# The cosine product of the keys' rotation: kept in PSUM, with the bank released by the sum

## The chip, the cores and the metric

The kernel runs on one core of a Trainium2 chip. The metric is the device time of one execution in microseconds; the median of three executions stands for the kernel. One execution was also taken with the hardware profiler, and all rows below are of that one.

## What is computed

The block is a gated cross-attention layer followed by a small expert layer. Only the first matters here. With `x` of 8 batches x 56 tokens x 512 and a context of 8 x 1500 x 512, it computes

```
q = layernorm(x) @ wq          # 32 heads of 128
k = context @ wk               # 8 key heads of 128, each shared by 4 query heads
v = context @ wv
q, k = rope(q), rope(k)        # rope(x) = x * cos + rotate_half(x) * sin
p = softmax(q @ k^T / sqrt(128) + mask)
x = x + tanh(g) * ((p @ v) @ wo)
```

`rotate_half` swaps the two halves of 64 of a head's 128 numbers; the sign sits in the sine table. So for each batch and each key head the kernel needs `k * cos + swapped(k) * sin` on 128 x 1500 numbers, the head's dimension on the partitions and the context's positions on the columns. All is in fp32.

## The kernel before, in words

**Precision by halves.** Each fp32 operand of a matmul is split in a high part (a rounded copy) and a low part (the rest). A product is three matmuls: high x high, low x high, high x low (`PASSES`). So every tensor that TensorE reads needs a copy by ACT (the high part) and a subtraction by DVE or POOL (the low part).

**Stages.** First the queries of all heads are computed and written to DRAM. Then comes the attention stage, which takes most of the time: 8 batches x 8 key heads ("groups"). At last the output projection and the expert layer.

**One step of the attention stage** handles group g of batch b. TensorE does the scores of group g (`S0` to `S5`: two halves of the query rows x three chunks of 500 positions), the transposes of the probabilities (`T0` to `T5`), their product with the values (`PV0` to `PV5`), and between them, for the next group, the keys (`K00` to `K23`: three chunks, each in four parts of three matmuls) and parts of the values (`V..`). In the last group of a batch, the "turn", the context of the next batch is transposed too (`C0` to `C11`).

The order of the pieces is written out by hand, one string for each engine: `PE_STEP`, `ACT_STEP`, `DVE_STEP`, each with a form for even groups (0, 2, 4, 6), odd groups (1, 3, 5), the turn (7), the last step of all, and the first keys. The engines run through their own strings in order and meet only at semaphores. In eight batches there are 32 even steps, 24 odd steps and 7 turns.

**The keys of one chunk** (an "item"; 3 per group, numbered through the whole kernel, `s` is the item's number modulo 2):

1. TensorE (`k_part`, line 805) makes twelve matmuls into PSUM bank `k_banks[:, s]`. There are two such banks (`RING = 2`), so item n uses the bank of item n-2. Ahead of an item's first matmul stands `pe.wait_ge(k_free, item + 1)`.
2. ACT (`k_exchange`, line 715) copies the two halves of the bank, swapped, to `k_swap[:, s]` in SBUF.
3. DVE (`k_cos_part`, line 938) multiplies the bank by the cosine table into `k_rot[:, s]` in SBUF, and signals `k_free`: from here on the bank may be written again. Since it writes `k_rot[:, s]`, it first waits until POOL has read that buffer for item n-2 (`k_lo`).
4. DVE (`k_sin_part`, line 942) multiplies `k_swap[:, s]` in place by the sine table.
5. DVE (`k_rotate`, line 948) adds the two in SBUF, and signals `k_rotated`.
6. ACT (`k_high`, line 720) makes the high part, POOL (`k_low`, line 673) the low part. The scores of the next step (line 845) wait for `k_lo`.

In the profile both `k_swap` and `k_rot` bear the name of the buffer that holds them, `k_work`; the key banks, the score banks and the value banks are all called `low_banks`.

In the strings, `K20` is the first part of chunk 2, so it is the one that reuses the bank of the same group's chunk 0. On TensorE it stands behind `K13` in odd steps (`... K11 K12 K13 K20 ...`), behind `K13 V40` in even ones and behind `K12 K13 T0 T1` in the turn. On DVE the words `cos0 sin0 rot0` are the three operations of chunk 0.

**The query part** rotates its queries in another way (lines 503, 505 and 508): the cosine product is written in place into its PSUM bank, and the sum reads that bank and the sine product in SBUF.

**The output projection** reuses the key banks; its first piece (`O0`) waits for the last keys' bank.

Of the kernel before, what the change touches and what calls it, by code (L numbers as in the profile page):

```python
# [27 lines left out]
SC = 500  # L28
NC = SK // SC
# [8 lines left out]
RING = 2  # L38
# [51 lines left out]
DVE_STEP = {  # L90
# [11 lines left out]
def step_kind(g, last):  # L102
    return ("last" if last else "turn") if g == HKV - 1 else ("odd" if g % 2 else "even")
# [6 lines left out]
def tasks(order):  # L110

    for word in order.split():
        what = word.rstrip("0123456789")
        digits = word[len(what):]
        numbers = tuple(int(x) for x in digits) if what in ("K", "V") else (int(digits),) if digits else (0,)
        yield what, numbers
# [7 lines left out]
def t_place(kind, what, n):  # L124

    fills = t_fills(PE_STEP, kind)
    assert fills == t_fills(ACT_STEP, kind) == t_fills(DVE_STEP, kind)
    assert t_fills(ACT_STEP, "pre") == t_fills(ACT_STEP, "even")
    return fills.index((what, n))
# [7 lines left out]
def k_item(b, g, c=0):  # L137

    return b * K_ITEMS + g * NC + c


def sv_item(b, g, i=0):

    return b * SV_ITEMS + (V_AHEAD + (g // 2) * (2 * SCORES + VT) + (g % 2) * (SCORES + V_REST) + i)


def v_fill(g, m):

    return m - (0 if g % 2 else V_AHEAD)
# [7 lines left out]
def c_item(b, m):  # L157

    return b * T_ITEMS + (NT + (HKV - 1) * PT + t_place("turn", "C", m))
# [367 lines left out]
def attention_part(nc, ctx, query, shared, cT, ctx_in, mask, wo, q_dram, inv_dram, attn_dram):  # L527
    ident, stage, w, tables, mask_t = shared.ident, shared.stage, shared.w, shared.tables, shared.mask_t
# [8 lines left out]
    def sem(name):  # L537
        return ctx.enter_context(nc.semaphore(name))

    def halves(name, shape):  # L540
# [5 lines left out]
    k_swap, k_rot = (shared.k_work[:, n * 2 * SC:(n + 1) * 2 * SC].rearrange("p (s n) -> p s n", s=2) for n in range(2))  # L546
# [11 lines left out]
    k_banks, sv_banks = shared.low_banks[:, 0:RING], shared.low_banks[:, RING:2 * RING]  # L558
# [2 lines left out]
    q_loaded = [sem(f"q_loaded{i}") for i in range(2)]  # L561
    sp_passed, dve_passed = sem("sp_passed"), sem("dve_passed")
    sv_ready, sv_free, v_hi = sem("sv_ready"), sem("sv_free"), sem("v_hi_ready")
    k_ready, k_swapped, k_free, k_sined, k_rotated, k_hi, k_lo = (
        sem(n) for n in ("k_ready", "k_swapped", "k_free", "k_sined", "k_rotated", "k_hi_ready", "k_lo_ready"))
    t_ready, t_hi, t_free = sem("t_ready"), sem("t_hi_ready"), sem("t_free")
    o_ready, o_lo_copied, o_free, attn_ready = sem("o_ready"), sem("o_lo_copied"), sem("o_free"), sem("attn_ready")
    inv_stored, inv_loaded = sem("inv_stored"), sem("inv_loaded")
# [227 lines left out]
    def _(pe):  # L796
        def k_part(item, s, g, c, d, context_item):

            if d == 0:
                pe.wait_ge(k_free, item + 1)  # L800
                if context_item is not None:

                    pe.wait_ge(t_free, context_item + (RING + 1))
            for n, (a, m) in enumerate(PASSES):
                mm = nc.tensor.matmul(k_banks[:, s, 0:SC], w[0][a][:, d, g * DH:(g + 1) * DH],  # L805
                                      cT[m][:, d, c * SC:(c + 1) * SC], start=(d == 0 and n == 0),
                                      stop=(d == DC - 1 and n == len(PASSES) - 1))
            if d == DC - 1:
                mm.then_inc(k_ready, 1)

        def v_part(item, g, m, t, context_item):

            if t == 0:
                pe.wait_ge(sv_free, item + 1)
            if context_item is not None:

                pe.wait_ge(t_free, context_item + (RING + 1))
            tile = 2 * m + t
            for d in range(DC):
                for n, (a, mv) in enumerate(PASSES):  # L820
                    mm = nc.tensor.matmul(sv_banks[0:ST, m % 2, t * PAIR:(t + 1) * PAIR],  # L821
                                          cT[a][:, d, tile * ST:(tile + 1) * ST], w[1][mv][:, d, g * DH:g * DH + PAIR],
                                          start=(d == 0 and n == 0), stop=(d == DC - 1 and n == len(PASSES) - 1))
            if t == 1:
                mm.then_inc(sv_ready, 1)

        def c_transposes(b, item, s, m):

            pe.wait_ge(t_free, item + 1)
            c_stage_ready(pe, b, m)  # L830
            for d in range(DC):
                mm = nc.tensor.transpose(t_banks[:, s, d * ST:(d + 1) * ST], c_tile(m)[:, d * P:(d + 1) * P],
                                         ident[0:ST, 0:ST])
            mm.then_inc(t_ready, 1)

        def scores(b, g, i):

            h, c = divmod(i, NC)
            if i == 0:
                pe.wait_ge(q_lo, b * HKV + (g + 1))  # L840
            pe.wait_ge(sv_free, sv_item(b, g, i) + 1)
            if h == 0:
                pe.wait_ge(k_lo, k_item(b, g, c) + 1)
            for n, (a, m) in enumerate(PASSES):
                mm = nc.tensor.matmul(sv_banks[0:ROWS, i % 2, 0:SC], q[a][:, h * ROWS:(h + 1) * ROWS],  # L845
                                      k[m][:, c * SC:(c + 1) * SC], start=(n == 0), stop=(n == len(PASSES) - 1))
            mm.then_inc(sv_ready, 1)

        def transposes(b, g, s, j, last):
            pe.wait_ge(t_free, t_item(b, g, j, last) + 1)  # L850
            if j == 0:

                pe.wait_ge(p_ready, b * (HKV * HALVES) + (g + 1) * HALVES)
            for t in range(2):
                for h in range(HALVES):
                    col = t * GQ + h * ROWS
                    mm = nc.tensor.transpose(t_banks[0:ST, s, col:col + ROWS],  # L857
                                             prob[h][:, (2 * j + t) * ST:(2 * j + t + 1) * ST], ident[0:ROWS, 0:ROWS])
            mm.then_inc(t_ready, 1)
# [33 lines left out]
        def step(b, g, last):  # L893
            kind = step_kind(g, last)
            turn = kind == "turn"
            for what, n in tasks(PE_STEP[kind]):
                if what in ("C", "T"):
                    t_bank = t_place(kind, what, *n) % 2
                if what == "S":
                    scores(b, g, *n)  # L900
                if what == "K":
                    k_part(k_item(b, g + 1, n[0]), ((g + 1) * NC + n[0]) % 2, (g + 1) % HKV, *n,
                           c_item(b, (n[0] + 1) * CT - 1) if turn else None)
                if what == "V":
                    v_part(sv_item(b, g, SCORES + v_fill(g, n[0])), (g + g % 2) % HKV, *n,
                           c_item(b, 2 * n[0] + n[1]) if turn else None)
                if what == "C":
                    c_transposes(b + 1, c_item(b, *n), t_bank, *n)
                if what == "T":
                    transposes(b, g, t_bank, *n, last)  # L910
                if what == "PV":
                    weigh(b, g, *n, last)
                if what == "O":
                    if n[0] == 0:

                        pe.wait_ge(k_free, k_item(b, g, NC - 1) + (RING + 1))
                        pe.wait_ge(sv_free, sv_item(b, g, SCORES - 1) + (RING + 1))
                    project_group(nc, pe, shared, n[0], n[0], n[0] == 0)

        for b in range(B - 1):  # L920
            for g in range(HKV):
                step(b, g, False)
        for g in range(HKV):
            step(B - 1, g, True)

    @block.vector
    def _(dve):
        for ring in (k_free, sv_free, t_free, o_free):
            dve.sem_inc(ring, RING)
        nc.vector.memset(o_sum[:, :], 0.0).then_inc(blank, 1)  # L930
        nc.vector.memset(inv_b[:, :], 1.0).then_inc(blank, 1)
        def k_cos_part(item, s, c):

            dve.wait_ge(k_swapped, item * 2 + 2)
            if not isinstance(item, int) or item >= 2:

                dve.wait_ge(k_lo, item - 1)
            nc.vector.tensor_tensor(k_rot[:, s], k_banks[:, s, 0:SC], tables[:, 0, c * SC:(c + 1) * SC],
                                    ALU.mult).then_inc(k_free, 1)

        def k_sin_part(s, c):
            nc.vector.tensor_tensor(k_swap[:, s], k_swap[:, s], tables[:, 1, c * SC:(c + 1) * SC],
                                    ALU.mult).then_inc(k_sined, 1)

        def k_rotate(item, s):
            dve.wait_ge(k_free, item + (RING + 1))
            dve.wait_ge(k_sined, item + 1)
            nc.vector.tensor_tensor(k_rot[:, s], k_rot[:, s], k_swap[:, s], ALU.add).then_inc(k_rotated, 1)

        def c_low(item, s, m):  # L950
            dve.wait_ge(t_hi, item + 1)
# [466 lines left out]
```

## Time and profile before

| what | value |
|---|---|
| median of 3 runs | 2008.38 us (2006.62 to 2009.34) |
| span of the profiled execution | 2005.4 us |
| TensorE (PE) busy | 1976.7 us, 99% |
| its weight loads (PEld) | 1775.9 us, 89% |
| VectorE (DVE) busy | 1235.0 us, 62% |
| ScalarE (ACT) busy | 1034.3 us, 52% |
| GpSimd (POOL) busy | 311.6 us, 16% |
| mean granted TensorE clock | 0.996 of full |

Times are microseconds from the span's start. A row of the timeline begins with the start and the duration; engine and source line follow, then the operation, what it writes `<-` what it reads, and the shapes. `x2` at the end means that two instructions are merged in the row. A bracket holds the idle time of the engine just before the instruction and what ended it. PE is a matmul and PEld the load of its weights, which runs under the matmul before it. Ends of matmuls are modelled, so matmuls that follow each other overlap in the rows; their starts are the better measure. DVE's rows also overlap by some 0.08 us when nothing is waited for.

### The profile page before, as it was taken

Reading aid. Unit: us, or ns where it says so; the run is one execution under the profiler, and the core shown is the slowest. Engines: PE = TensorE matmul, PEld = TensorE weight load, DVE = VectorE, ACT = ScalarE, POOL = GpSimd, SP = SyncE. Lnnn points to the kernel's source line nnn. Section 1 sums busy time; section 2 is a strip of 40 time slices with the busy share of each in tenths; the row PEclk is TensorE's granted clock in tenths of the full one; section 3 lists DMA queues with packets and bytes.
Section 4 is the critical chain, followed back from the end, with each engine's and each line's share of the span. In section 5 each row is a group of like instructions: output and inputs, shape, how many; then the busy total and the mean of one; then the engine's idle time right before and its main releaser. Section 6 shows DMA issues by size and latency. Waiting matters only on the chain. (4 is left out here: it accounts for less than half of the span.)

```text
span 2005.4 us, 32965 instructions
## 1 busy us (share of the span) xinstructions
PE 1976.7 (99%) x12404; PEld 1775.9 (89%) x12404; DVE 1235.0 (62%) x2639; ACT 1034.3 (52%) x1754; POOL 311.6 (16%) x227
## 2 busy tenths in 40 slices
PE   7999999999999999999999999999999999999998
PEld 7989889988899988998899988998899998999786
DVE  6766556666666666666666666666665666566544
ACT  6655555554545555555644555455554555455532
POOL 5511111111111111111111111111111111111200
PEclk9999999999999999999999999999999999999998
DMA  7611212111211212221111112221111112121270
GB/s 227 248 56 35 35 18 44 35 31 20 43 10 33 36 17 44 35 35 20 39 19 25 35 20 41 36 35 20 39 25 26 28 20 41 36 33 15 48 263 19
DMA packets 74904, 94.41 MB, mean 47 GB/s; under 512 B 22692, under 2 KB 49444, under 8 KB 74760
## 3 DMA queue, kind: packets, MB, share of 16 engines
q1 hardware_dynamic: 73752, 86.01, 20.4%
q10 hardware_dynamic: 1008, 6.42, 0.8%
q8 instruction: 97, 1.59, 0.4%
q14 instruction: 47, 0.39, 0.1%
HBM read 76.64 MB, written 15.77 MB: 46 GB/s over the span
## 5 line engine op out<-in xcount | busy, mean ns | idle before, releaser
L673 POOL TENSOR_TENSOR k_lo<-k_work,k_hi 128x500 fp32r<-128x500 f32 x192 | 244.1, 1285 | 1541.0 <-ACT k_hi L720 1513.3
L821 PE MATMUL low_banks<-wv_hi,cT_hi 128*125 128x256 f32 x1536 | 443.1, 288 | 0.0
L821 PE MATMUL low_banks<-wv_hi,cT_lo 128*125 128x256 f32 x1536 | 431.0, 281 | 0.0
L821 PE MATMUL low_banks<-wv_lo,cT_hi 128*125 128x256 f32 x1536 | 430.9, 281 | 0.0
L1027 DVE TENSOR_TENSOR pT<-t_banks,pT 125x448 fp32r<-125x448 f32 x384 | 236.0, 622 | 242.8 <-ACT pT L785 242.8
L1002 DVE CUSTOM_DVE_ANT_0 prob<-low_banks,mask_t 112x500 f32<-112x500 f32 x384 | 259.1, 678 | 178.2 <-PE low_banks L845 176.9
L785 ACT ACTIVATE pT<-t_banks 125x448 fp32r<-125x448 f32 x384 | 205.1, 543 | 309.2 <-PE t_banks L857 308.2
L760 ACT ACTIVATE prob<-prob,neg_max 112x1500 f32<-112x1500 f32 x128 | 198.6, 1552 | 289.7 <-DVE neg_max L1007 288.9
L805 PE MATMUL low_banks<-cT_hi,wk_hi 128*128 128x500 f32 x768 | 312.0, 406 | 0.0
L805 PE MATMUL low_banks<-cT_hi,wk_lo 128*128 128x500 f32 x768 | 298.6, 389 | 0.0
L805 PE MATMUL low_banks<-cT_lo,wk_hi 128*128 128x500 f32 x768 | 298.3, 388 | 0.0
L821 PEld LDWEIGHTS low_banks<-wv_hi,cT_hi 128*125 128x125 f32 x1536 | 285.1, 186 | 4.3
L821 PEld LDWEIGHTS low_banks<-wv_hi,cT_lo 128*125 128x125 f32 x1536 | 285.8, 186 | 2.7
L821 PEld LDWEIGHTS low_banks<-wv_lo,cT_hi 128*125 128x125 f32 x1536 | 285.2, 186 | 0.0
L874 PE MATMUL o_banks<-pT,v_hi 125*128 125x448 f32 x768 | 272.4, 387 | 1.8 <-DVE pT L1027 0.7
L715 ACT ACTIVATE k_work<-low_banks 64x500 f32<-64x500 f32 x384 | 223.6, 582 | 14.4 <-PE low_banks L805 5.8
L857 PE MATMUL t_banks<-ident,prob 112*125 112x112 f32 x1536 | 220.6, 270 | 0.9 <-DVE pT L1027 0.9
L857 PEld LDWEIGHTS t_banks<-ident,prob 112*125 112x125 f32 x1536 | 207.0, 188 | 14.3 <-DVE pT L1027 1.0
L962 DVE TENSOR_TENSOR v_lo<-low_banks,v_hi 125x512 fp32r<-125x512 f32 x192 | 132.2, 689 | 137.0 <-ACT v_hi L734 137.0
L734 ACT ACTIVATE v_hi<-low_banks 125x512 fp32r<-125x512 f32 x192 | 114.3, 595 | 192.5 <-PE low_banks L821 192.3
L874 PE MATMUL o_banks<-pT,v_lo 125*128 125x224 f32 x768 | 193.5, 265 | 0.0
L805 PEld LDWEIGHTS low_banks<-cT_lo,wk_hi 128*128 128x128 f32 x768 | 144.5, 188 | 29.9
(136 smaller groups left out, 2910.2 us busy)
## 6 DMA issues: line engine op xcount, KB each, us to landing
stage<-in_ctx_dram SPq DMA_DIRECT2D x72, 250.0 KB
attn_by_head<-attn SPq DMA_DIRECT2D x65, 112.0 KB, 1.7
wq_raw<-in_L_xattn_wq_dram SPq DMA_DIRECT2D x7, 1024.0 KB, 7.2
q_raw<-q_by_head SPq DMA_DIRECT2D x64, 112.0 KB, 4.9
inv_b<-inv_by_head SPq DMA_DIRECT2D x64, 112.0 KB, 5.1
head_rows<-in_ctx_dram SPq DMA_DIRECT2D x24, 250.0 KB
mask_t<-in_mask_BxSxS_ff_dram SPq DMA_DIRECT2D x16, 328.1 KB
stage<-in_L_xattn_wo_dram SPq DMA_DIRECT2D x4, 1024.0 KB, 7.3
```

Source lines behind the costliest of these rows:

```text
L673: nc.gpsimd.tensor_tensor(k[1][:, c * SC:(c + 1) * SC], k_rot[:, s], f32(k[0][:, c * SC:(c + 1) * SC]), ALU.subtract).then_inc(k_lo, 1)
L715: nc.scalar.activation(k_swap[lo * HALF:(lo + 1) * HALF, s], k_banks[(1 - lo) * HALF:(2 - lo) * HALF, s, 0:SC], ACT.Copy).then_inc(k_swapp ...
L734: nc.scalar.activation(v[0][:, 2 * m:2 * m + 2, :], sv_banks[0:ST, m % 2, :].rearrange("p (t n) -> p t n", t=2), ACT.Copy).then_inc(v_hi, 1)
L760: nc.scalar.activation(prob[n][:, :], prob[n][:, :], ACT.Exp, bias=neg_max[:, n:n + 1], accum_out=row_sum[:, n:n + 1]).then_inc(p_ready, 1)
L785: nc.scalar.activation(pT[:, n % PT_SLOTS, :, 0, :], t_banks[0:ST, t_bank, 0:2 * GQ].rearrange("p (t n) -> p t n", t=2), ACT.Copy).then_in ...
L805: mm = nc.tensor.matmul(k_banks[:, s, 0:SC], w[0][a][:, d, g * DH:(g + 1) * DH], cT[m][:, d, c * SC:(c + 1) * SC], start=(d == 0 and n == ...
L821: mm = nc.tensor.matmul(sv_banks[0:ST, m % 2, t * PAIR:(t + 1) * PAIR], cT[a][:, d, tile * ST:(tile + 1) * ST], w[1][mv][:, d, g * DH:g * ...
L857: mm = nc.tensor.transpose(t_banks[0:ST, s, col:col + ROWS], prob[h][:, (2 * j + t) * ST:(2 * j + t + 1) * ST], ident[0:ROWS, 0:ROWS])
L874: mm = nc.tensor.matmul(o_banks[:, g % 2, 0:(2 - a) * GQ], v[a][:, 2 * j + t, (g % 2) * DH:(g % 2 + 1) * DH], probs, start=(first and a == ...
L962: nc.vector.tensor_tensor(v[1][:, 2 * m:2 * m + 2, :], sv_banks[0:ST, m % 2, :].rearrange("p (t n) -> p t n", t=2), f32(v[0][:, 2 * m:2 * ...
L1002: nc.vector.tensor_tensor_reduce(prob[h][:, c * SC:(c + 1) * SC], sv_banks[0:ROWS, n % 2, 0:SC], mask_t[:, c * SC:(c + 1) * SC], 1.0, LOWE ...
L1027: nc.vector.tensor_tensor(pT[:, n % PT_SLOTS, :, 1, :], t_banks[0:ST, t_bank, 0:2 * GQ].rearrange("p (t n) -> p t n", t=2), f32(pT[:, n % ...
```

## The change

The cosine product is written back into its own PSUM bank, and its semaphore is now called `k_cosined`. The sum reads the bank and `k_swap`, and writes `k_rot`. The bank is released by the sum: the first matmul of item n waits for `k_rotated` of item n-2, and the first two items wait for nothing. The wait for POOL's low part of item n-2 moves from the cosine product to the sum. In the odd steps' DVE order `rot0` moves ahead of `inv` (the reciprocals of the row sums) and `T0`. The output projection's first piece waits for the last `k_rotated`.

```diff
@@ DVE_STEP
-    "odd": ("mask0 mask1 mask2 max0 mask3 mask4 mask5 max1 norm cos0 sin0 inv T0 rot0 T1 T2 cos1 V0 sin1 rot1 T3 T4 Q V1 "
+    "odd": ("mask0 mask1 mask2 max0 mask3 mask4 mask5 max1 norm cos0 sin0 rot0 inv T0 T1 T2 cos1 V0 sin1 rot1 T3 T4 Q V1 "
             "cos2 T5 sin2 V2 rot2 V3 out"),
@@ k_part, on TensorE
             if d == 0:
-                pe.wait_ge(k_free, item + 1)
+                if item >= RING:
+                    pe.wait_ge(k_rotated, item - RING + 1)
...
@@ output projection, on TensorE
-                        pe.wait_ge(k_free, k_item(b, g, NC - 1) + (RING + 1))
+                        pe.wait_ge(k_rotated, k_item(b, g, NC - 1) + 1)
...
@@ on DVE
-        for ring in (k_free, sv_free, t_free, o_free):
+        for ring in (sv_free, t_free, o_free):
             dve.sem_inc(ring, RING)
...
         def k_cos_part(item, s, c):
             dve.wait_ge(k_swapped, item * 2 + 2)
-            if not isinstance(item, int) or item >= 2:
-                dve.wait_ge(k_lo, item - 1)
-            nc.vector.tensor_tensor(k_rot[:, s], k_banks[:, s, 0:SC], tables[:, 0, c * SC:(c + 1) * SC],
-                                    ALU.mult).then_inc(k_free, 1)
+            nc.vector.tensor_tensor(k_banks[:, s, 0:SC], k_banks[:, s, 0:SC], tables[:, 0, c * SC:(c + 1) * SC],
+                                    ALU.mult).then_inc(k_cosined, 1)
...
         def k_rotate(item, s):
-            dve.wait_ge(k_free, item + (RING + 1))
+            dve.wait_ge(k_cosined, item + 1)
             dve.wait_ge(k_sined, item + 1)
-            nc.vector.tensor_tensor(k_rot[:, s], k_rot[:, s], k_swap[:, s], ALU.add).then_inc(k_rotated, 1)
+            if item >= 2:
+                dve.wait_ge(k_lo, item - 1)
+            nc.vector.tensor_tensor(k_rot[:, s], k_banks[:, s, 0:SC], k_swap[:, s], ALU.add).then_inc(k_rotated, 1)
```

## Rows read from the trace of the kernel before

**Rows 1.** Page, shares of busy time, and the slices.

```profile
PE 1976.7 (99%) x12404; PEld 1775.9 (89%) x12404; DVE 1235.0 (62%) x2639; ACT 1034.3 (52%) x1754; POOL 311.6 (16%) x227
...
PE   7999999999999999999999999999999999999998
...
PEclk9999999999999999999999999999999999999998
```

**Rows 2.** Waits, whole span: us in total, times, longest.

```profile
PEld o_banks L874 <- DVE pT L1027: 10.9, 33, 0.9
...
DVE k_work L938 <- POOL k_lo L673: 5.8, 24, 0.2
```

**Rows 3.** Groups of instructions by form: busy us, mean ns, idle before.

```profile
L938 DVE TENSOR_TENSOR k_work<-low_banks,k_tables 128x500 f32<-128x500 f32 x192 | 129.0, 672 | 40.3 <-ACT k_work L715 32.8 <-POOL k_lo L673 5.8
...
L505 DVE TENSOR_TENSOR q_banks<-q_banks,q_cos_t 128x448 f32<-128x448 f32 x32 | 19.9, 623 | 0.0
...
L508 DVE TENSOR_TENSOR q_rot<-q_banks,q_sine 128x448 f32<-128x448 f32 x16 | 10.0, 624 | 2.4 <-DVE q_banks L505 1.0
```

**Rows 4.** The sum's line (948): duration in ns, least, median, most.

```profile
L948 DVE TENSOR_TENSOR k_work<-k_work x192: 666/678/900, 111.8 to 1879.4; 128x500 f32<-128x500 f32 x192
```

**Rows 5.** Timeline, first odd step (batch 0, group 1), around K20.

```profile
156.59 0.67 DVE L938 TENSOR_TENSOR k_work<-low_banks,k_tables 128x500 f32<-128x500 f32 x1
...
157.17 0.67 DVE L942 TENSOR_TENSOR k_work<-k_work,k_tables 128x500 f32<-128x500 f32 x1
...
157.58 0.19 PEld L805 LDWEIGHTS low_banks<-cT_hi,wk_hi 128*128 128x128 f32 x1
...
158.02 0.39 PE L805 MATMUL low_banks<-cT_hi,wk_lo 128*128 128x500 f32 x1
...
160.35 0.62 DVE L1027 TENSOR_TENSOR pT<-t_banks,pT 125x448 fp32r<-125x448 f32 x1 [2.16 <-ACT pT L785]
...
160.89 0.67 DVE L948 TENSOR_TENSOR k_work<-k_work 128x500 f32<-128x500 f32 x1
```

**Rows 6.** Timeline, last of the 24 odd steps.

```profile
1835.88 0.67 DVE L942 TENSOR_TENSOR k_work<-k_work,k_tables 128x500 f32<-128x500 f32 x1
1836.28 0.19 PEld L805 LDWEIGHTS low_banks<-cT_hi,wk_hi 128*128 128x128 f32 x1
```

**Rows 7.** Timeline, first of the 32 even steps.

```profile
133.80 0.68 DVE L948 TENSOR_TENSOR k_work<-k_work 128x500 f32<-128x500 f32 x1
...
134.48 0.19 PEld L805 LDWEIGHTS low_banks<-cT_hi,wk_hi 128*128 128x128 f32 x1
...
134.83 0.38 PE L805 MATMUL low_banks<-cT_hi,wk_lo 128*128 128x500 f32 x1
```

**Rows 8.** Timeline, first and last of the 7 turns.

```profile
328.15 0.19 PEld L805 LDWEIGHTS low_banks<-cT_hi,wk_hi 128*128 128x128 f32 x1
...
328.99 0.67 DVE L942 TENSOR_TENSOR k_work<-k_work,k_tables 128x500 f32<-128x500 f32 x1
...
329.76 0.68 DVE L948 TENSOR_TENSOR k_work<-k_work 128x500 f32<-128x500 f32 x1
...
1673.33 0.19 PEld L805 LDWEIGHTS low_banks<-cT_hi,wk_hi 128*128 128x128 f32 x1
...
1675.08 0.68 DVE L948 TENSOR_TENSOR k_work<-k_work 128x500 f32<-128x500 f32 x1
```

**Rows 9.** Timeline of the last batch's end; two stretches with TensorE's granted clock.

```profile
1880.84 0.61 DVE L1027 TENSOR_TENSOR pT<-t_banks,pT 125x448 fp32r<-125x448 f32 x1
...
1881.50 0.19 PEld L874 LDWEIGHTS o_banks<-pT,v_hi 125*128 125x128 f32 x1 [0.95 <-DVE pT L1027]
...
1881.82 0.38 PE L874 MATMUL o_banks<-pT,v_lo 125*128 125x224 f32 x2
...
1885.28 0.45 PE L845 MATMUL low_banks<-k_hi,q_hi 128*112 128x500 f32 x1 [2.19 <-POOL k_lo L673]
...
1880.00:1890.00 10.00, 6.83 (x26) 4.34 (x25) 4.65 (x13) 4.37 (x6) 10.00 (x9) 0.86 0.32 82
1890.00:1897.00 7.00, 6.02 (x29) 5.08 (x28) 3.43 (x9) 5.16 (x6) 0.79 (x1) 0.96 0.57 200
```

The columns of the last two rows are: stretch, its length, busy time (and instructions) of PE, PEld, DVE, ACT and POOL, then the granted clock, the DMA engines' busy share and GB/s.

More of the change, by code:

```diff
@@ L563, in attention_part @@
     sv_ready, sv_free, v_hi = sem("sv_ready"), sem("sv_free"), sem("v_hi_ready")
-    k_ready, k_swapped, k_free, k_sined, k_rotated, k_hi, k_lo = (
-        sem(n) for n in ("k_ready", "k_swapped", "k_free", "k_sined", "k_rotated", "k_hi_ready", "k_lo_ready"))
+    k_ready, k_swapped, k_cosined, k_sined, k_rotated, k_hi, k_lo = (
+        sem(n) for n in ("k_ready", "k_swapped", "k_cosined", "k_sined", "k_rotated", "k_hi_ready", "k_lo_ready"))
     t_ready, t_hi, t_free = sem("t_ready"), sem("t_hi_ready"), sem("t_free")
```

## The prediction

> **What bounds the kernel now.** I read the shares of busy time first. TensorE is busy for 1976.7 of 2005.4 us, and in the 40 slices its share is 90% or more everywhere but in the first and the last; the granted clock is 9 tenths or more in all but the last [rows 1]. So most of the 28.7 us without TensorE work lies ahead of the attention stage or behind it, so a DVE instruction that gets quicker can give back next to nothing, while every wait added in front of a matmul is paid whole. Then the waits: over the whole span TensorE's queue waited 10.9 us for DVE's probability halves and had no wait at a key bank (no row names line 805 as the waiting one); DVE waited 5.8 us for POOL in front of the cosine product, 24 times [rows 2]. So the two key banks are no bound today. The question is how much room they have, and the wait table cannot tell it. For that I read the timeline at the first matmul of chunk 2 (K20), which reuses the bank of chunk 0.
>
> **The release moves from the cosine product to the sum.** Item n+2 of the keys writes the bank of item n. K20 is the tight one. The order on TensorE and on DVE is fixed, and each of the three kinds of step has its own distance.
>
> Durations first. The cosine product, which reads PSUM and writes SBUF, takes 672 ns at 500 columns, and the present sum, on SBUF alone, a median of 678 [rows 3, 4]; reading PSUM costs nothing. In the query part the forms of the change are there at 448 columns: in place in PSUM 623 ns, and a sum of a PSUM and an SBUF operand 624 [rows 3]. Scaled straight by the columns those are 695 and 696 at 500, 0.02 us more than now; if part of the time is fixed, as much as now. I take 0, and 0.04 us for the two instructions as the other end.
>
> *Odd steps, 24 of them* (three in each of eight batches). In the first one the cosine product ends at 156.59 + 0.67 = 157.26 and K20's weight load starts at 157.58, so today it has 0.32 us of room. Sine runs from 157.17 to 157.84, but the sum only at 160.89, since DVE first waits for the first probability tile at 160.35 [rows 5]. The change moves the sum ahead of the reciprocals and of that tile. It can start 0.11 us after sine, at 157.95 (in the turn step it is 329.66 to 329.76, in others 0.11 [rows 8]), and ends at 158.62. From DVE's end to a weight load held by it is 0.05 us (1880.84 + 0.61 = 1881.45, load at 1881.50) [rows 9]. The sum now has a third wait, for POOL's low half, behind the two; long satisfied, but a wait that must be passed. No row prices it: between 0 and the 0.11 us that two waits leave; I take 0.04. So K20's load starts at 158.71 in place of 157.58, 1.13 us later. A held load does not run under the matmul before it, but the flow behind it is closer: unheld, the second matmul starts 158.02 - 157.58 = 0.44 after the load [rows 5]; held, it was 1881.82 - 1881.50 = 0.32 in the tail [rows 9]. That gives 0.12 back, with the rounding 0.13: 1.00 us per odd step, 24.0 us. The last odd step stands as the first: sine ends at 1836.55, load at 1836.28, as 157.84 to 157.58 [rows 6].
>
> *Turn steps, 7.* Here the order on DVE is not changed, and the sum stands behind the first probability tile. It ends at 329.76 + 0.68 = 330.44, while K20's load starts at 328.15, with two transposes just ahead of it and so without the overlap above. Held until 330.53, that is 2.38 us; the last turn has 1675.76 against 1673.33 [rows 8]. 7 x 2.38 = 16.7 us.
>
> *Even steps, 32.* The sum ends at 134.48 and the load starts at 134.48. 0.05 for the signal and 0.04 for the third wait, less the overlap, here 134.83 - 134.48 = 0.35 against 0.32, so 0.02 or 0.03 [rows 7]: 0.07 each, 2.2 us.
>
> Together 42.9 us. Behind the held load stand, on TensorE, the rest of K20 to K23, the probability transposes and the value products, all in one queue; ACT's and DVE's next work waits for those, so the whole pattern moves along with TensorE, and what follows has no spare wait into which the delay could sink except the 10.9 us in [rows 2], which are local (a probability tile that TensorE itself made shortly before).
>
> **What costs nothing.** Chunk 0 of the next group reuses the bank of this group's chunk 1, and chunk 1 that of chunk 2. The sum of chunk 1 stands ahead of the last probability tile on DVE, for which TensorE waits anyway before it ends a step; the sum of chunk 2 stands ahead of the last value half, which the second score block waits for. Both are done when the key matmuls come. The reciprocals come 0.7 us later on DVE; the normalisation they feed is in the next step. The first probability tile of odd steps had 2.16 us of idle DVE ahead of it [rows 5], which covers the sum of 0.68. The wait for POOL's low half leaves the cosine product, and at the sum, two or more instructions later, it is met. If that cover were missing, DVE would lose what it lost before, 5.8 us [rows 2], off TensorE's path. The output projection's wait at the end goes to a sum that is long done.
>
> **The clock.** TensorE's granted clock fell once inside the work: after a wait of its loads of 0.95 us for DVE at 1881.50 and a gap of 2.19 us for POOL at 1885.28, the stretches 1880 to 1890 and 1890 to 1897 show 0.86 and 0.96. At 0.5 for part of them, that is (0.14 x 10 + 0.04 x 7) / 0.5 = 3.4 us at 1.2 GHz, so 1.7 us of work lost [rows 9]. Seven turn steps will have a gap of some 2.1 us, close to that one, though alone. I take four falls of seven: 6.8 us, with bounds of 0 and 7 x 1.7 = 11.9. The odd steps' 1.0 us is like the wait of 0.95 alone; I count no fall for it.
>
> Sum against the profiled execution: 2005.4 + 42.9 + 6.8 = 2055.1. That execution's span lies 3.0 us under the median of the runs, 2008.38; I add them: **2058 us**.
>
> **Rivals.**
> A. The delay is partly taken back: TensorE's present waits for DVE (10.9 us) vanish because DVE has caught up while TensorE stood still. For it: DVE is idle for much of the span, as each wait in [rows 2] says. Against: those waits are for tiles that TensorE itself made just before. With all of it gone and no fall of the clock: 2008.4 + 42.9 - 10.9 = 2040.
> B. Every stall, the odd ones too, is followed by 3.4 us at half clock: 31 x 1.7 = 52.7 in place of 6.8, 2104 us. For it: the odd stalls come to 1.0 us, and the one fall had a wait of 0.95 in front of it as well. Against: what followed it was the gap of 2.19, and the odd stalls stand alone.
> C. Faster: DVE and POOL get out of each other's way. The sum no longer reads two SBUF tensors, and DVE's 24 waits for POOL go (5.8 us [rows 2]); the sum falls from its median of 678 to its least of 666 ns, 192 x 0.012 = 2.3 us [rows 4]. For it: some sums took up to 900 ns, so something does meet them. To decide, the sum would have to end before K20's load, that is DVE be 1.1 us earlier in odd steps and 2.4 us in turns; from that point TensorE is unhindered and gains at most these 8.1 us: 2000. Against: cosine, sine and sum follow each other on one engine behind mask passes that wait for TensorE's scores, and the median sits 12 ns above the least, so meetings are rare.
>
> The rule beside this rival is the Trainium skill's (SBUF — State Buffer, section "Who interferes with whom"): a VectorE operation with two SBUF inputs and a GpSimd operation that reads SBUF exclude each other through a shared port pair, and a PSUM operand takes the sum out of that. By it the change would tend to be faster; this trace agrees only in the few long sums.
>
> D. The change does not hold TensorE: the transposes or value products before K20 come later than I read. With no stall and no gain, 2008.
>
> **How the numbers follow.** Forecast (stalls at K20, with 0 to 7 falls) 0.82; A 0.07; B 0.05; C 0.03; D 0.03. The forecast's own range: without the price of the third wait and with no fall it is 42.9 - 63 x 0.04 = 40.4, so 2049; with 0.11 for that wait (63 x 0.07 = 4.4), 0.04 more for the PSUM forms (2.5) and seven falls (5.1 more than four) it is 2058 + 12 = 2070. To leave no more than 2 in 10 out it reaches down over A: 2038 to 2070. Within 0.2% (4 us, about what a measurement of this kernel can tell from no change) falls D and some of C: 0.04; faster 0.02; slower 0.94.
>
> **What would show it.** In the changed kernel line 805's first load must appear among TensorE's waits, released by DVE's sum, in 24 + 7 places for 0.9 to 1.1 and 2.1 to 2.4 us, and barely in the 32 even ones. The distance from a batch to the next, now (1673.33 - 328.15) / 6 = 224.2 us [rows 8], grows by 3 x 1.00 + 2.38 + 4 x 0.07 = 5.7 to 229.9, and by 1.7 more where the clock falls. The sum in odd steps must start within 0.2 us of the sine's end. DVE's wait for POOL at the cosine product must be gone. The granted clock shows the falls, between none and seven. It is wrong if line 805 does not wait, if DVE reaches the cosine product of chunk 0 at another distance from TensorE's scores, or if the PSUM forms take more than 0.75 us.

## The result, and the profile after

The changed kernel takes 2055.12 us (median of four runs, 2051.58 to 2060.94) against 2008.54 us before: 1.0237 times the time, 95% interval 1.0225 to 1.0249, 47 us slower. The forecast was 2058, with a range of 2038 to 2070. The profiled execution has a span of 2059.2 us, 53.8 more than the profiled one before. One execution of 3898 us, of the kernel in the last experiment, is left out of its median.

The page, the rows that answer to [rows 1]; ACT's busy time hardly moved, POOL's fell by 3.8 us, and TensorE's share fell from 99 to 97%:

```profile
PE 1995.5 (97%) x12404; PEld 1782.7 (87%) x12404; DVE 1235.5 (60%) x2639; ACT 1034.6 (50%) x1754; POOL 307.8 (15%) x227
```

The waits, as in [rows 2]. A row that did not exist before is now TensorE's largest: the weight load of the keys' first matmul (line 807, before 805), released by DVE's sum (line 950, before 948). DVE's row for POOL at the cosine product is gone, the probability halves' row has hardly changed, and the context loads' row (1.6 us, 3 times before) has grown:

```profile
PEld low_banks L807 <- DVE k_work L950: 44.8, 33, 2.4
...
PEld o_banks L876 <- DVE pT L1029: 10.6, 33, 0.7
...
PE t_banks L834 <- DMA stage<-in_ctx_dram: 3.9, 5, 1.3
```

Two groups of instructions by form, as in [rows 3]: the in-place cosine product and the sum that reads PSUM.

```profile
L937 DVE TENSOR_TENSOR low_banks<-low_banks,k_tables 128x500 f32<-128x500 f32 x192 | 130.5, 679 | 35.4 <-ACT k_work L715 33.7
...
L950 DVE TENSOR_TENSOR k_work<-low_banks,k_work 128x500 f32<-128x500 f32 x192 | 129.6, 675 | 12.2 <-issue 0.9
```

The same timeline as [rows 5], first odd step. The sum now follows sine at once (158.08 + 0.67 = 158.75 to 158.84), ends at 159.52, and the held load starts 0.05 later. The bracket is the time that the weight loader stood idle:

```profile
157.49 0.68 DVE L937 TENSOR_TENSOR low_banks<-low_banks,k_tables 128x500 f32<-128x500 f32 x1
...
158.08 0.67 DVE L941 TENSOR_TENSOR k_work<-k_work,k_tables 128x500 f32<-128x500 f32 x1
...
158.84 0.68 DVE L950 TENSOR_TENSOR k_work<-low_banks,k_work 128x500 f32<-128x500 f32 x1
...
159.57 0.19 PEld L807 LDWEIGHTS low_banks<-cT_hi,wk_hi 128*128 128x128 f32 x1 [1.12 <-DVE k_work L950]
...
159.90 0.39 PE L807 MATMUL low_banks<-cT_hi,wk_lo 128*128 128x500 f32 x1
```

The first turn, as [rows 8]: the sum ends at 335.03, behind the first probability tile, and two transposes' worth of work does not cover it.

```profile
333.04 0.62 DVE L1029 TENSOR_TENSOR pT<-t_banks,pT 125x448 fp32r<-125x448 f32 x1 [0.80 <-ACT pT L785]
333.58 0.67 DVE L941 TENSOR_TENSOR k_work<-k_work,k_tables 128x500 f32<-128x500 f32 x1
334.35 0.68 DVE L950 TENSOR_TENSOR k_work<-low_banks,k_work 128x500 f32<-128x500 f32 x1
...
335.07 0.19 PEld L807 LDWEIGHTS low_banks<-cT_hi,wk_hi 128*128 128x128 f32 x1 [2.28 <-DVE k_work L950]
```

In the first even step, as [rows 7], the load has no bracket, and yet it starts 0.05 us behind the sum's end, as the held loads do. It is so in all 32 even steps. In the kernel before, where nothing tied the two together, the load started within 0.01 us of the sum's end:

```profile
134.66 0.68 DVE L950 TENSOR_TENSOR k_work<-low_banks,k_work 128x500 f32<-128x500 f32 x1
135.39 0.19 PEld L807 LDWEIGHTS low_banks<-cT_hi,wk_hi 128*128 128x128 f32 x1
```

The clock, stretches behind four of the seven turns' holds; the columns are those of the stretches in [rows 9], and the third number from the end is the granted clock. It fell at six of the seven; the fourth turn (1030) is the exception:

```profile
566.00:571.00 5.00, 4.49 (x14) 3.80 (x15) 1.70 (x5) 0.50 (x2) 0.00 (x0) 0.66 0.03 0
799.00:804.00 5.00, 5.00 (x21) 4.25 (x20) 0.72 (x2) 0.00 (x0) 0.00 (x0) 0.66 0.07 3
1030.00:1034.00 4.00, 4.00 (x24) 3.55 (x23) 0.86 (x2) 0.26 (x1) 0.00 (x0) 1.00 0.03 0
...
1492.00:1497.00 5.00, 5.00 (x17) 4.16 (x18) 1.13 (x3) 0.00 (x0) 0.00 (x0) 0.66 0.03 0
```

A fall is 0.34 x 5 / 0.5 = 3.4 us at 1.2 GHz instead of 2.4 GHz, 1.7 us of work. On TensorE it costs a little less: the last matmul of K23 starts 8.25 us after the last one of K13 in the turn at 566, and 6.69 in the fourth turn, which had no fall.

**Where the 53.8 us went.** The terms are worked out from the starts of the matmuls, in every step of the two traces. The delay of a step is how much later K21 (the next part of the same chunk) starts after the last matmul of K13; what the falls of the clock add has a row of its own:

| term | us |
|---|---|
| 24 odd steps: K20 starts 1.11 after the matmul before it instead of 0.22; the matmul after it then 0.33 instead of 0.22; 0.99 to 1.00 each | 23.9 |
| two of them 1.47 instead of 1.11, since DVE started late | 0.7 |
| 7 turns: held for 2.33, the last one for 2.45; the matmul after it 0.02 later | 16.5 |
| 32 even steps: two late by 0.2 and 0.3, the others by 0.02 to 0.04 | 1.2 |
| six falls of the clock in turns, 1.4 to 1.6 each | 9.1 |
| longer waits for the context loads in the turns (3.9 against 1.6) | 2.3 |
| the query part, ahead of all this (K20 of the first even step, 135.47 - 134.60) | 0.9 |
| sum | 54.6 |

At the last key matmul the changed kernel is 54.4 us behind the kernel before. From there to the end of the span it takes 0.7 us less, which gives the 53.8 found; that last piece is not explained.

### The profile page after: what moved, and what is told of

The parts are those of the page before. It is cut to its first block and busy times, and to the rows that moved or that the text cites. A ratio compares the mean times of both kernels' runs of the same rounds, so it can differ in the third digit from the quotient of the medians.

```text
span 2059.2 us, 32772 instructions
## 1 busy us (share of the span) xinstructions
PE 1995.5 (97%) x12404; PEld 1782.7 (87%) x12404; DVE 1235.5 (60%) x2639; ACT 1034.6 (50%) x1754; POOL 307.8 (15%) x227
## 5 line engine op out<-in xcount | busy, mean ns | idle before, releaser
L807 PE MATMUL low_banks<-cT_hi,wk_hi 128*128 128x500 f32 x768 | 318.0, 414 | 33.0 <-DVE k_work L950 33.0
L807 PEld LDWEIGHTS low_banks<-cT_hi,wk_hi 128*128 128x128 f32 x768 | 146.6, 191 | 66.6 <-DVE k_work L950 44.8
```

## The experiments

Two bases are used: the kernel before and the changed kernel. My theory was that nothing but the later release of the bank costs time, that it does so at K20, and that the turns' holds let the clock fall. The rivals were a price of the PSUM operands or of the moved wait, a clock that falls for all holds together, and a hold that is set by something other than DVE's order.

### Late release alone, with the operands left in SBUF

```diff
 kernel before
+ the odd DVE order of the change
-                pe.wait_ge(k_free, item + 1)
+                if item >= RING:
+                    pe.wait_ge(k_rotated, item - RING + 1)
```

> Kernel before, with the odd DVE order of the change and with TensorE's wait for the sum instead of the cosine product; the cosine product still goes to SBUF and the sum still reads SBUF alone. Theory (the hold of K20 until the sum is the whole cost): the same as the changed kernel, 2051 to 2061 us by the number of clock falls, with 1.1 us waits of the weight load in odd steps and 2.3 in turns. Rival (the operands in PSUM, or the moved wait for POOL's low half, cost part of it): some us less, down to 2035.

Measured: 2059.09 us (2056.47 to 2063.24; ratio 1.0262, interval 1.0245 to 1.0279). The wait is there in full, and DVE's wait for POOL has come back with the old place of its semaphore:

```profile
PEld low_banks L806 <- DVE k_work L949: 44.8, 31, 2.4
...
DVE k_work L939 <- POOL k_lo L673: 5.8, 24, 0.2
```

The delays of K20, taken as in the table above, are 25.0 us in odd steps, 16.6 in turns and 1.6 in even steps, 43.2 together; in the changed kernel they are 24.6, 16.5 and 1.2, together 42.3. So keeping the product in PSUM costs nothing and earns at most 1 us; the semaphore costs the rest. The rival is out: this kernel isn't faster than the changed one, and its interval overlaps with it. The clock fell at four turns in the profiled execution.

### The odd DVE order alone

```diff
 kernel before
-    max1 norm cos0 sin0 inv T0 rot0 T1 T2 cos1 ...
+    max1 norm cos0 sin0 rot0 inv T0 T1 T2 cos1 ...
```

> Kernel before, with only the odd DVE order of the change (sum ahead of the reciprocals and the first probability tile). Theory: 2008, within 0.1%, since the sum fills idle DVE time. Rival (the order itself delays the reciprocals and the tile enough to be felt): 24 x 0.3 us or more, 2015.

Measured: 2008.32 us (ratio 1.0002, interval 0.9992 to 1.0011), as the theory had it.

### The late release in the turns only

```diff
 kernel before
-                pe.wait_ge(k_free, item + 1)
+                if item % K_ITEMS == 2 and item >= K_ITEMS:
+                    pe.wait_ge(k_rotated, item - RING + 1)
+                else:
+                    pe.wait_ge(k_free, item + 1)
```

> Kernel before, with TensorE's wait for the sum only at K20 of the 7 turn steps. Theory: 7 x 2.35 = 16.4 us for the hold, and 1.7 us for each fall of the clock, none to seven: 2025 to 2037, and runs that differ from each other by multiples of 1.7. Rival (falls come from all stalls together, not from the turn's alone): 2025, one fall as before.

Measured: 2032.05 us (2030.01 to 2036.18; ratio 1.0125, interval 1.0109 to 1.0142), 24.0 us more than before. The seven holds are 16.5 us of it. The rest, 7.5 us, is the clock: the trace shows five falls at turns (mean clock 0.991), of 1.5 us each. The row of waits has exactly the seven:

```profile
PEld low_banks L808 <- DVE k_work L951: 16.1, 7, 2.4
```

The rival, that all holds together make the clock fall, is out: no odd step is held here.

### The late release in the odd steps only

```diff
 kernel before
+ the odd DVE order of the change
-                pe.wait_ge(k_free, item + 1)
+                if item % K_ITEMS in (8, 14, 20):
+                    pe.wait_ge(k_rotated, item - RING + 1)
+                else:
+                    pe.wait_ge(k_free, item + 1)
```

> Kernel before, with the odd DVE order of the change and TensorE's wait for the sum only at K20 of the 24 odd steps. Theory: 24 x 0.98 = 23.5 us and no further fall of the clock: 2032, with runs close together. Rival (odd stalls make the clock fall too): 2045 to 2070.

Measured: 2033.98 us (2033.35 to 2034.71; ratio 1.0130, interval 1.0114 to 1.0147), 25.9 more than before where 23.5 was expected. No fall beyond the one at the end (mean clock 0.996), so holds of 1 us do not disturb it. Three of the 24 holds are longer, because DVE paused between sine and the sum. The timeline of one:

```profile
840.98 0.67 DVE L945 TENSOR_TENSOR k_work<-k_work,k_tables 128x500 f32<-128x500 f32 x1
842.11 0.68 DVE L951 TENSOR_TENSOR k_work<-k_work 128x500 f32<-128x500 f32 x1 [0.46 <-DVE k_work L945]
842.84 0.19 PEld L808 LDWEIGHTS low_banks<-cT_hi,wk_hi 128*128 128x128 f32 x1 [1.50 <-DVE k_work L951]
```

21 x 0.99 + 3 x 1.35 = 24.8, and 25.0 if each step is taken from its rows. The profiled execution is 26.9 us longer than the profiled one before; of the rest, 1.6 us lie ahead of the first keys and 0.8 in one longer wait for the context. Both vary from trace to trace, and the median need not have them.

Turns alone and odd steps alone add up to 49.9 us; with all steps released late, as above, it was 51.0. The 1.6 us of the even steps are in that one only.

### The normalisation behind the sum

```diff
 changed kernel, odd DVE order
-    max1 norm cos0 sin0 rot0 inv T0 ...
+    max1 cos0 sin0 rot0 norm inv T0 ...
```

> Changed kernel; in DVE's odd order the normalisation (0.39 us, one every 0.31) moves from ahead of the cosine product of chunk 0 to behind its sum. Theory (K20 is held until the sum, so each tenth of DVE work ahead of the sum counts on TensorE): 24 x 0.31 = 7.4 us less than the changed kernel, 2048, and the odd wait of the weight load 0.8 in place of 1.1. Rival (the hold is set by something else, such as the swap or the scores): 2055.

Measured: 2043.38 us (2041.54 to 2044.16; ratio 1.0172, interval 1.0155 to 1.0189). That is 11.7 us less than the changed kernel, 4.3 more than I allowed. The odd wait has shrunk, from 1.12 to 0.79 in the first odd step and from 1.14 to 0.79 in most others:

```profile
160.08 0.68 DVE L950 TENSOR_TENSOR k_work<-low_banks,k_work 128x500 f32<-128x500 f32 x1
...
160.81 0.19 PEld L807 LDWEIGHTS low_banks<-cT_hi,wk_hi 128*128 128x128 f32 x1 [0.79 <-DVE k_work L950]
```

That is 0.36 us in most steps where 0.31 was expected. With one late DVE start in place of two, the delays of the 24 odd steps went from 24.6 to 15.7 us, 9.0 less. The rest, 2.7 us, is the clock: it fell at one turn in the profiled execution, though the seven turns' holds are the same to 0.01 us (K20 3.47 after K13). The stretches behind the first two:

```profile
335.00:340.00 5.00, 4.71 (x15) 3.96 (x16) 1.48 (x5) 0.28 (x2) 0.00 (x0) 0.66 0.07 3
565.00:570.00 5.00, 4.18 (x23) 3.67 (x24) 1.92 (x5) 0.89 (x3) 0.00 (x0) 1.00 0.03 0
```

### Value work between K13 and K20 in odd steps

```diff
 changed kernel, odd TensorE order
-    ... K13 K20 K21 T0 K22 T1 K23 T2 PV0 V00 T3 V01 ...
+    ... K13 V00 K20 K21 T0 K22 T1 K23 T2 PV0 T3 V01 ...
```

> Changed kernel; in TensorE's odd order the value part V00 (12 matmuls, 1.4 us) moves from behind PV0 to between K13 and K20, as in even steps. Theory: the odd hold of 1.1 us is covered, 24 us less: 2031 (2026 to 2037 by the number of clock falls), no wait of the weight load in odd steps. Rival (the delay comes back at the next tile, as T3 now follows PV0 at once): up to 24 x 0.5 of it back, 2043.

Measured: 2032.30 us (2031.99 to 2034.48; ratio 1.0123, interval 1.0106 to 1.0140). The sum ends at 158.83, and K20's load, now behind 12 value matmuls, comes at 159.32 without a wait:

```profile
158.15 0.68 DVE L950 TENSOR_TENSOR k_work<-low_banks,k_work 128x500 f32<-128x500 f32 x1
...
159.32 0.19 PEld L807 LDWEIGHTS low_banks<-cT_hi,wk_hi 128*128 128x128 f32 x1
```

V00 costs no time in its new place: K20 comes 1.44 us later after K13 than in the kernel before, and the next step begins with that time given back (1.43). What is left is the turns' part; the result is that of the turn-only kernel (2032.05) from the other side. The clock fell at five turns in the profiled run.

### Another DVE order in the turn

```diff
 changed kernel, DVE order of the turn
-    ... cos0 C10 C11 T0 sin0 rot0 inv ...
+    ... cos0 C10 C11 sin0 rot0 T0 inv ...
```

> Changed kernel; in DVE's turn order sine and sum of chunk 0 move ahead of the first probability tile. Theory: the turn's hold falls from 2.33 to 0.94 us, 7 x 1.39 = 9.7 us, and the clock no longer falls in the turns, which takes 1.7 us for each fall from the mean: 2040, and runs within 2 us of each other. Rival (falls come from the number of stalls, not the length of the turn's): 2045 with runs spread over 9 us as now.

Measured: 2038.99 us (2038.17 to 2039.68; ratio 1.0154, interval 1.0137 to 1.0171), runs 1.5 us apart, and no fall of the clock in any turn of the trace (mean clock 0.996 in all four executions). The fall near the end lasted 6.8 us in this trace and 3.4 in all others; why is not known. The load waits 0.85 in place of 2.28 us:

```profile
331.34 0.68 DVE L950 TENSOR_TENSOR k_work<-low_banks,k_work 128x500 f32<-128x500 f32 x1
332.07 0.19 PEld L807 LDWEIGHTS low_banks<-cT_hi,wk_hi 128*128 128x128 f32 x1 [0.85 <-DVE k_work L950]
```

### No hold at all

```diff
 changed kernel
+ V00 between K13 and K20 in odd steps
+ the other DVE order in the turn
 TensorE order of the turn
-    ... K12 K13 T0 T1 K20 K21 K22 PV0 K23 T2 V00 T3 ...
+    ... K12 K13 T0 T1 V00 K20 K21 K22 PV0 K23 T2 T3 ...
```

> Changed kernel with the V00 move of odd steps, the DVE turn order of the other run, and V00 between T1 and K20 in the turn as well. Theory: no hold of K20 is left, the time is that of the kernel before, 2008 (2007 to 2011). Rival (the PSUM operands or the later release cost something beyond K20): 2012 or more.

Measured: 2009.29 us (2007.72 to 2010.12, ten runs; ratio 1.0005, interval 0.9995 to 1.0015). With K20 covered in odd steps and turns the change is nearly free, and no more than that. What the wait table still shows are two even steps:

```profile
PEld low_banks L807 <- DVE k_work L950: 0.4, 2, 0.2
```

The even steps are not covered, though. Their loads start 0.05 us behind the sum's end, as in the changed kernel, and their delays add up to 1.5 us.

### The wait for POOL back at the cosine product

```diff
 kernel without a hold
 k_cos_part
+            if not isinstance(item, int) or item >= 2:
+                dve.wait_ge(k_lo, item - 1)
 k_rotate
-            if item >= 2:
-                dve.wait_ge(k_lo, item - 1)
```

> The kernel without a hold of K20 (V00 moved, turn order changed), with the wait for POOL's low half put back from the sum to the cosine product. Theory (this wait is off TensorE's path): the same 2009.3 us within 0.1%, and DVE's 5.8 us of waiting for POOL there again. Rival: slower by up to 5.8 us.

Measured: 2009.38 us (ratio 1.0005, interval 0.9996 to 1.0014), the same as without it. DVE's wait is there again and nobody feels it (the even steps' delays are 1.6 us here):

```profile
DVE low_banks L939 <- POOL k_lo L673: 6.0, 24, 0.6
```

### All orders on the kernel before

The diff is that of the kernel without a hold, applied to the orders of the kernel before, whose release and operands stay.

> Kernel before, with all the orders of the kernel without a hold (odd DVE order, V00 ahead of K20 in odd steps and turns, turn DVE order), early release and SBUF operands kept. Theory: the orders and the operands are both free where K20 is covered, so this is the same as the kernel before and as the one without a hold, 2008 to 2009.3. Rival (the later release or the PSUM operands still cost 1 to 2 us): 2006 to 2007.5, below the kernel without a hold.

Measured: 2007.70 us (ratio 0.9999, interval 0.9990 to 1.0008). The kernel without a hold lies 1.6 us above it, the one with the wait for POOL put back 1.7. All three intervals hold 1.0000, so the times alone leave it open whether the change costs a last microsecond. The traces say that it does: the even steps' delays are 0.0 us in this kernel, against 1.5 and 1.6 in those two, which have the same orders and the late release. The last of the 32 even steps, in the kernel with the wait for POOL put back:

```profile
1870.21 0.68 DVE L949 TENSOR_TENSOR k_work<-low_banks,k_work 128x500 f32<-128x500 f32 x1
...
1870.95 0.19 PEld L807 LDWEIGHTS low_banks<-cT_hi,wk_hi 128*128 128x128 f32 x1
```

No version ran measurably faster than the kernel before.

## Why the prediction was right

**The bound.** TensorE being the only engine without room was right, and so was looking at the distance of K20's load from the release rather than at the wait table: that table had no row for the bank, though the room was only 0.32 us in odd steps.

**Odd steps.** Forecast 24.0 us, in the trace 23.9 + 0.7. The single estimates held: 0.11 from sine to the sum (measured 0.09 to 0.10), 0.05 from DVE's end to the load, 0.13 back behind a held load (0.22 + 0.22 unheld against 0.33 held). The third wait that the sum got was counted 0.04 and costs nothing: 158.75 to 158.84 with three waits, 0.11 with two. What made up for it can be placed in part: the cosine product begins 0.98 ahead of K13's last matmul instead of 0.99 and takes 0.68 instead of 0.67, and so does the sum. The two late DVE starts (0.7 us) were not in the forecast.

**Turns.** Forecast 16.7 (2.38 each), measured 16.5: 2.33 in six turns, where the difference is again the third wait, and 2.45 in the last, in which the kernel before went from K13 to K20 in 1.02 us instead of 1.14.

**Even steps.** Forecast 2.2, measured 1.2. The mechanism was right: the load now starts 0.05 behind the sum's end in all 32. 0.04 of the 0.07 was the third wait; the other 0.03 is what most steps show (0.02 to 0.04), and two steps with a late DVE add 0.5. This is the part that covering K20 in odd steps and turns does not take away.

**The clock.** Forecast four falls of seven at 1.7 us, 6.8 us; six in the profiled execution, 9.1 us, since a fall costs 1.5. The number four was a choice between none and seven, so that it came out near the middle of the four runs is luck. The four runs have mean clocks of 0.991, 0.992, 0.995 and 0.995 at 2060.94, 2056.59, 2053.66 and 2051.58 us. One fall lowers the mean clock by 0.5 x 3.4 / 2055 = 0.0008, so with 0.996 for the end alone these are about six, five, one and one. This is most of the spread of the changed kernel (five falls more are 7.6 us, and the spread is 9.4), and it is why the median is 2055 and not 2061. For the median the terms give 24.6 + 16.5 + 1.2 + 3.25 x 1.5 = 47.2 us, an estimate with the mean number of falls; 46.6 were measured and 49.7 forecast. That a gap of 2.1 us alone would do what the cluster in [rows 9] did was an inference from one case; it held for four to six of the seven turns in four traces, and for one of seven in the normalisation experiment.

**The rest.** 2.3 us of longer context loads and 0.9 us of the query part were not in the sum. They belong to this execution: the context wait is 1.5 to 2.7 us in the traces of the ten experiments, and their first keys start between 0.7 us earlier and 2.5 us later than those of the kernel before.

**The batch distance.** The sign that was asked for, 224.2 us growing to 229.9 and by a fall more where the clock falls, came as (1723.24 - 335.07) / 6 = 231.4 from the first turn's load to the last's. The steps make 5.5 of the 7.2 more, the five falls in between 1.3 and the context waits 0.4.

**The rivals.** A (delay taken back by waits that shrink) did not happen: the row of the probability halves went from 10.9 to 10.6. B (falls after odd holds) is refuted by the odd-only kernel. C (DVE and POOL out of each other's way) had its mechanism and not its price: DVE's 5.8 us of waits went, and the longest sum fell from 900 ns [rows 4] to 680, POOL's longest low half from 1787 to 1280; that this saves TensorE any time, no run shows:

```profile
L950 DVE TENSOR_TENSOR k_work<-low_banks,k_work x192: 668/678/680, 112.5 to 1933.9; 128x500 f32<-128x500 f32 x192
```

The port rule of the Trainium skill (SBUF — State Buffer, "Who interferes with whom") agrees with that: the long ones are gone once the sum has an operand in PSUM. There was one long sum, and seven long low halves of POOL, one in each turn, and each of the eight is a sum and a POOL instruction that run at the same time. Another timing of the same work is not the reason. The last two experiments have the same orders, and their sums meet POOL at the same eight places; with both operands of the sum in SBUF (first pair of rows, the fifth turn) POOL takes 1.78 us, with one in PSUM (second pair) 1.28:

```profile
1242.39 0.67 DVE L948 TENSOR_TENSOR k_work<-k_work 128x500 f32<-128x500 f32 x1
1242.40 1.78 POOL L673 TENSOR_TENSOR k_lo<-k_work,k_hi 128x500 fp32r<-128x500 f32 x1 [9.53 <-ACT k_hi L720]
...
1244.58 0.67 DVE L949 TENSOR_TENSOR k_work<-low_banks,k_work 128x500 f32<-128x500 f32 x1
1244.59 1.28 POOL L673 TENSOR_TENSOR k_lo<-k_work,k_hi 128x500 fp32r<-128x500 f32 x1 [9.52 <-ACT k_hi L720]
```

The long ones are there in all six traces with the sum's operands in SBUF, late release or not, and in none of the six with one in PSUM. So the rival's mechanism is real, and it is met only eight times in 192. D is out by the first wait row.

## What to carry to other kernels

A buffer that shows no wait can still be the tightest one. Before moving a release to a later instruction, take the distance from the present release to the user's first instruction, the weight load and not the matmul, in every kind of step; the wait table can't give it. Nor does a missing bracket mean that nothing holds the load: in even steps it started 0.05 us behind the sum's end 32 times, which cost 1.2 to 1.6 us in all. A release that moves by n instructions of an in-order engine costs all of those instructions, including the ones of other tasks that stand between (here a probability tile in the turn), wherever the bound engine comes first. And such a hold can be covered at no cost by putting work that the bound engine has to do anyway between the two, as the value part did.

## What the runs showed of the hardware that I had not expected

- The same hold of 2.1 us on TensorE made the granted clock fall from 2.4 to 1.2 GHz for 3.4 us at six, five, four or one of the seven turns, depending on the trace. By the mean clocks it differs between runs of the changed kernel (about six, five, one and one falls), and it was 0.994 to 0.995 in all four runs of the normalisation experiment, 0.991 to 0.992 in all four with the value part moved. Gaps of 0.7 us between matmuls (24 odd steps, and the turns with the other DVE order), and the few of 1.1, never did it. So a gap of 2.1 us costs its own time and up to 1.6 us more. Why one execution has six falls and another one, with the same gaps, no run here shows.
- DVE sometimes starts an instruction 0.35 us late with nothing to wait for, three times in 24 odd steps of the odd-only kernel and at the same three steps of the late-release kernel (850.38 and 842.85, for example, are K20 of the same step). It was hidden before; on TensorE's path it counts. What it is has not been tried, but the traces have a trail. In the attention stage of the odd-only kernel there are seven such late starts, and behind each of them, 0.6 to 1.0 us later, a transfer of 8 KB on the queue of kind "instruction" (q14) begins: 842.11 and 842.8, 1125.31 and 1126.0, 1408.47 and 1409.1 are the three in odd steps. Counted by DVE's own instructions, the seven lie multiples of 256 apart. That suggests the loading of DVE's code; no run changed it.
- A third, long satisfied semaphore wait in front of a DVE instruction cost nothing that the trace can show (0.09 to 0.10 us from sine to the sum with three waits, 0.11 with two). An in-place fp32 product in PSUM took 679 ns where the one that writes SBUF takes 672.
